# A hand-written interleaving of two transformer layers: where the second layer's feed-forward input, the first layer's gating and one state update stand in the order of work

## The chip, the cores and the metric

The kernel runs on one core of a Trainium2 chip. The metric is the time of one execution in device microseconds (us). A core has a matrix engine (PE, with its weight loads shown apart as PEld), a vector engine (DVE), an activation engine (ACT), a general engine (POOL) and DMA queues that the sync engine (SP) fills. Each engine works through its own list of instructions in order and waits on semaphores for the others.

## The reference

Eight sequences of 512 tokens with 128 features pass through two layers. Cut to what matters:

```python
x = L0_attn_x                                   # (8, 512, 128)
xn = layernorm(x)
s = causal_attention(xn)                        # 16 heads of 8, latent keys and values
g = silu(expert_ffn(xn))                        # 8 experts of 64, top 2 by gate
x = x + s * g
xn = layernorm(x)                               # called xn2 in the kernel
h = layernorm(xn) * gamma + beta                # called hn
k, v, q = h @ Wk.T + bk, h @ Wv.T + bv, h @ Wq.T + bq
# scan over the 512 tokens, W starts at 0:
#   y_t = W q_t ;  W = W - 0.01 * (W k_t - v_t) k_t^T
s = xn + y
g = silu(xn @ sign(weight).T)
x = x + s * g
```

The scan is done in four chunks of 128 tokens per sequence, each with a triangular inverse.

## The kernel before, in words

**Stages.** Up to five sequences are in work at once. In one iteration of the schedule one sequence (`second`) is normed and projected, the next (`nxt`) has its score maxima taken, the third (`cur`) has its attention done, the fourth (`prev`) goes through the second layer, and the fifth (`older`) is finished and stored. An iteration has four groups of ten units, written (group, unit) here, from (0, 0) to (3, 9), and a short group 4. A unit is an `s_unit` for `nxt` (scores into one half of `ps_s`, which DVE reduces to maxima in `cand`) and then an `e_unit` for `cur` (scores into one half of `ps_e`, which ACT exponentiates into `prob`). Each of `ps_s` and `ps_e` has two halves, so that unit n needs the `cand` (or `prob`) of unit n-2 to be finished.

**Order.** Between the units the table `PLAN` places all other pieces by hand. Every engine walks the same table and issues its own part of each piece, so that a piece's place sets its rank on all engines at once. `iteration` walks the table, `schedule` strings the iterations together, `numbers` counts the uses of a shared accumulator bank in that order, and the waits on `a_`, `c0_` and `c1_` semaphores come from these counts. Steady iterations are those in which `cur` is sequence 1 to 6; the last one has its own table, `LAST_PLAN`.

**Pieces that are touched.** `gb0` to `gb3`: PE spreads the gates (line 858, bank `ps_a`) and DVE multiplies the hidden activations by them (line 1441). `out`: 20 matmuls of the expert output (lines 865 and 867, `ps_a`), then ACT's tanh into `tG` (line 1238) and DVE's product (line 1446). `gt`: PE transposes the gates' parts, which POOL makes (lines 634 to 640) from DVE's `gate` (line 1436). `hn_norm` and `xn2_norm`: four DVE operations each (line 1394). `c_xn2t`: PE transposes `xn2` (line 969), ACT copies it out (line 1262). `c_ffn`: PE multiplies it by the sign weights (line 1074), ACT takes a tanh (line 1308), DVE finishes (line 1547). `c_vk`: PE projects values and keys into both banks `ps_c0` and `ps_c1` (line 997). `c_u2`: PE makes the third chunk's update (line 1099), ACT copies it into `u_sb` (line 1313), and `c_y2` uses it (line 1109). `pv0` to `pv2`: PE's product of probabilities and values for a group (line 950). `gelu`: ACT loads another function table and works over all of `hid` (line 1234); the next `prob` needs the first table again (line 1251). `ln2_stats` and `c_y3`: DVE's statistics and the last sum of the older sequence (lines 1377, 1382 and 1593). `c_out` on POOL: gate and add for the older sequence (lines 687 and 691).

Of the kernel before, what the change touches and what calls it, by code (L numbers as in the profile page):

```python
# [53 lines left out]

C0_PIECES = ("c_kt", "c_vk", "c_gram", "lev_a1", "lev_a2", "lev_a3", "lev_a4", "lev_a5", "lev_a6",
             "lev_d1", "lev_d2", "lev_d3", "lev_d4", "lev_d5", "c_u0", "c_u1", "c_u2", "c_u3", "c_r1", "c_r2", "c_r3", "c_y0", "c_y1", "c_y2")
C1_PIECES = ("c_ht", "c_qt", "c_vk", "c_gram", "c_xn2t", "c_ffn", "lev_d5", "lev_d6", "c_y3")


PLAN = {  # L60
    (0, 0): ["c_u3"], (0, 1): ["gb0"], (0, 2): ["ln2_stats", "c_y3"], (0, 4): ["ln2_rstd", "hn_norm"],
    (0, 6): ["pv0"], (0, 7): ["c_ht", "rn", "c_out"], (0, 8): ["gb1"], (0, 9): ["pv1", "c_kt", "c_qt"],
    (1, 0): ["load_x", "m_rows1"], (1, 1): ["c_vk", "gb2"], (1, 2): ["c_gram", "pv2"], (1, 3): ["logits"],
# [6 lines left out]
}  # L70
# [126 lines left out]
def two_layers(nc, x_in, W_dq, W_uq, W_dkv, W_uk, W_uv, W_o, w1_in, b1_in, w2_in, b2_in, cent_in, route_in,  # L197
               Wk_in, bk_in, Wv_in, bv_in, Wq_in, bq_in, gamma_in, beta_in, sign_in, out):
    SEQS, TOK, D = x_in.shape
    NT = TOK // P  # L200
# [5 lines left out]
    with ExitStack() as ctx:  # L206
# [299 lines left out]
        def _(pool):  # L506
# [112 lines left out]
            def token_norms(b):  # L619

                pool.wait_ge(S["ss_ready"], b.count(2, 2))
                g.tensor_scalar(ssm[:, :], ss[:, :], float(P), NORM_EPS * NORM_EPS, ALU.mult, ALU.max).then_inc(S["ssm_ready"], 1)
                pool.wait_ge(S["ssm_ready"], b.count(1, 1))
                after(pool, S["norm2"], NT * (b.c - 1))
                after(pool, S["cos_ready"], b.count(1, 0))
                g.tensor_tensor(rn[:, :], ssm[:, :], halfpow[:, 0, :], ALU.pow).then_inc(S["rn_ready"], 1)
# [53 lines left out]
            def c_out(b):  # L680
                r, o = second_layer(b)
                if b.c == SEQS - 1:
                    return
                pool.wait_ge(r.S["c1_emptied"], C1_NUMBER[b.c, "c_y3"] + 1)
                if b.c < SEQS - 2:
                    pool.wait_ge(r.S["c0_emptied"], C0_NUMBER[b.c + 1, "c_kt"] + 1)
                g.tensor_tensor(r.syg[:, :, :], r.sy[:, :, :], r.tF[:, :].rearrange("p (i d) -> p i d", i=NT), ALU.mult)\  # L687
                    .then_inc(r.S["syg_ready"], 1)
                pool.wait_ge(r.S["syg_ready"], o.count(1, 1))
                after(pool, r.S["stored"], o.count(16, 0))  # L690
                g.tensor_tensor(r.out_sb[:, :, :], x1[b.parity][:, :, :], r.syg[:, :, :], ALU.add).then_inc(r.S["out_ready"], 1)
# [26 lines left out]
        def _(pe):  # L718
# [245 lines left out]
            def c_xn2t(b):  # L964
                r, o = second_layer(b)
                c1_fill(b, "c_xn2t")
                pe.wait_ge(r.S["norm1"], o.count(NT, NT))
                for i in range(NT):
                    last = tr(r.ps_c1[:, tok(i)], r.xn2[:, i, :], ident[:, :])
                last.then_inc(r.S["c1_filled"], 1)  # L970

# [98 lines left out]
            def c_ffn(b):  # L1070
                r, o = second_layer(b)
                c1_fill(b, "c_ffn")
                for i in range(NT):
                    last = mm(r.ps_c1[:, tok(i)], r.xn2T[:, tok(i)], sgT[:, :], start=True, stop=True)
# [60 lines left out]
        def _(act):  # L1135
# [123 lines left out]
            def c_xn2t(b):  # L1259
                r, o = second_layer(b)  # L1260
                c1_full(b, "c_xn2t")
                copy(r.xn2T[:, :], r.ps_c1[:, :]).then_inc(r.S["c1_emptied"], 1)

# [379 lines left out]
```

## Time and profile before

| | |
|---|---|
| median of 3 runs | 617.68 us (611.39 to 619.85) |
| the profiled execution | 617.68 us, of which the span of instructions is 616.0 us |
| PE busy | 580.8 us, 94% |
| DVE busy | 391.8 us, 64% |
| ACT busy | 351.9 us, 57% |
| POOL busy | 171.7 us, 28% |
| mean granted TensorE clock | 0.982 |

A busy share counts the time in which at least one instruction of the engine is in work. The profiled execution is the median one, and 1.7 us of it lie outside its span. Times in the trace are counted from the start of the span. The unit (0, 0) of the steady iteration that serves as the example below starts its `e_unit` at 251.0 us, the next iteration's at 318.4 us.

### The profile page before, as it was taken

What the parts mean: (1) busy time and instruction counts of PE and PEld (TensorE: products, weight loads), DVE (VectorE), ACT (ScalarE), POOL (GpSimd) and SP (SyncE); (2) the same over time, 40 slices, a digit from 0 to 9 for tenths busy, and PEclk for the clock granted to TensorE, in tenths of its full rate; (3) what the DMA queues carried; (4) which work ended last, traced back from release to release, by engine and by line L of the source; (5) the groups of instructions that cost most, each with busy time, mean ns of one, the idle gap of its engine ahead of it and who ended that gap; (6) DMA issues with size and microseconds to landing.
All of it is one profiled execution on the core that took longest, in us unless ns stands there. A gap on an engine that the chain in (4) does not pass through costs nothing.

```text
span 616.0 us, 17485 instructions
## 1 busy us (share of the span) xinstructions
PE 580.8 (94%) x7289; PEld 389.4 (63%) x7289; DVE 391.8 (64%) x975; ACT 351.9 (57%) x679; POOL 171.7 (28%) x335
## 2 busy tenths in 40 slices
PE   7799989899998999899999999899998999799897
PEld 3345564567575766677666766678576777565565
DVE  4488765767667676867666685767666675412453
ACT  4412556755675476756675466656675476676231
POOL 7157022412224221432223230432224200311121
PEclk9999999999998999999998999799998999999899
DMA  4766293847252115410362014410361000000001
GB/s 113 162 153 132 44 84 90 157 63 63 74 116 48 43 29 114 97 43 10 87 118 60 10 45 98 95 44 5 83 128 41 10 12 1 26 18 2 3 3 35
DMA packets 58163, 39.42 MB, mean 64 GB/s; under 512 B 17957, under 2 KB 57988, under 8 KB 58084
## 3 DMA queue, kind: packets, MB, share of 16 engines
q1 hardware_dynamic: 58051, 38.29, 30.9%
q8 instruction: 58, 0.95, 0.7%
q14 instruction: 22, 0.17, 0.1%
q10 hardware_dynamic: 32, 0.01, 0.0%
HBM read 24.46 MB, written 9.96 MB: 56 GB/s over the span
## 4 chain that ended last, share of the span: by engine, by line
PE 79%; DVE 11%; ACT 4%; issue 2%; DMA 1%; POOL 1%; SPq 0%; DVEq 0%; POOLq 0%
PE ps_v L950 13%; PE ps_s L930 11%; PE ps_e L911 6%; PE ps_a L865 5%; PE ps_a L851 4%; PE ps_c L1015 4%; DVE cand L1457 4%; PE ps_e L903 3%; PE ps_e L907 3%; PE ps_e L738 3%; PE ps_a L820 3%; PE ps_s L933 2%; PE ps_c L1099 1%; PE ps_c L997 1%; PE ps_c L984 1%
## 5 line engine op out<-in xcount | busy, mean ns | idle before, releaser
L1457 DVE TENSOR_REDUCE cand<-ps_s 128x4 f32<-128x512 f32 (+1 forms) x320 | 213.4, 685 | 74.4 <-PE ps_s L933 45.4
L1251 ACT ACTIVATE prob<-ps_e 128x512 f32<-128x512 f32 x320 | 188.4, 598 | 97.2 <-PE ps_e L911 55.7
L930 PE MATMUL ps_s<-kst,qst 72*128 72x128 bf16 (+2 forms) x1024 | 126.4, 236 | 15.8 <-DVE cand L1457 12.0
L930 PEld LDWEIGHTS ps_s<-kst,qst 72*128 72x128 bf16 (+1 forms) x1024 | 72.1, 98 | 77.5 <-DVE cand L1457 36.5
L911 PE MATMUL ps_e<-qst,kst 75*128 75x256 bf16 (+3 forms) x416 | 105.3, 284 | 0.0
L950 PE MATMUL ps_v<-prob,vaug 128*32 128x512 f32 (+3 forms) x1024 | 90.6, 455 | 0.0
L903 PE MATMUL ps_e<-identb,negmask 128*128 128x150 bf16 (+3 forms) x320 | 73.2, 229 | 3.7 <-ACT prob L1251 3.3
L907 PE MATMUL ps_e<-qst,kst 128*128 128x128 bf16 x384 | 75.8, 223 | 0.0
L911 PEld LDWEIGHTS ps_e<-qst,kst 75*128 75x128 bf16 x416 | 40.9, 98 | 3.5
L738 PE MATMUL ps_e<-identb 128*128 128x512 bf16 x115 | 40.5, 408 | 1.9 <-POOL identb L520 1.9
L907 PEld LDWEIGHTS ps_e<-qst,kst 128*128 128x128 bf16 x384 | 38.4, 100 | 4.6 <-issue 0.3
L903 PEld LDWEIGHTS ps_e<-identb,negmask 128*128 128x128 bf16 x320 | 31.5, 99 | 14.6 <-ACT prob L1251 9.8
L950 PEld LDWEIGHTS ps_v<-prob,vaug 128*32 128x32 f32 x1024 | 24.1, 109 | 25.9 <-issue 20.3
L933 PE MATMUL ps_s<-negmask,identb 128*128 128x300 bf16 (+1 forms) x128 | 40.3, 315 | 0.0
L1015 PEld LDWEIGHTS ps_c<-second 32*32 32x32 f32 x2072 | 25.0, 107 | 21.3 <-issue 15.8
L649 POOL CAST mparts<-nm 128x32 bf16<-128x32 f32 x16 | 3.4, 211 | 121.8 <-DVE nm L1464 121.8
L865 PEld LDWEIGHTS ps_a<-w2s,hid 128*128 128x128 f32 x256 | 31.1, 192 | 7.1 <-issue 5.9
L1015 PE MATMUL ps_c<-second 32*32 32x32 f32 x2072 | 32.8, 194 | 2.5 <-DVE second L1520 1.6
L851 PE MATMUL ps_a<-xnT,w1s 128*128 128x512 f32 x64 | 33.5, 605 | 1.3 <-ACT hid L1230 0.8
L865 PE MATMUL ps_a<-w2s,hid 128*128 128x128 f32 x256 | 33.4, 283 | 0.7 <-ACT mrow L1243 0.7
L1230 ACT ACTIVATE hid<-ps_a,vecT 128x512 f32<-128x512 f32 x32 | 22.0, 687 | 17.1 <-PE ps_a L851 17.1
L687 POOL TENSOR_TENSOR second<-second,second_flat 128x512 f32<-128x512 f32 x7 | 8.9, 1266 | 60.2 <-ACT second_flat L1272 46.3
(340 smaller groups left out, 929.9 us busy)
## 6 DMA issues: line engine op xcount, KB each, us to landing
qst<-q_scratch SPq DMA_DIRECT2D x48, 192.0 KB
kst<-k_scratch SPq DMA_DIRECT2D x48, 192.0 KB
q_scratch<-qparts SPq DMA_DIRECT2D x24, 128.0 KB, 2.3
k_scratch<-kparts SPq DMA_DIRECT2D x24, 128.0 KB, 2.3
x_res<-in_L_attn_x_dram SPq DMA_DIRECT2D x8, 256.0 KB, 3.7
xn<-in_L_attn_x_dram SPq DMA_DIRECT2D x7, 256.0 KB, 3.5
out_dram<-second SPq DMA_DIRECT2D x7, 256.0 KB, 2.4
max_scratch<-mrow SPq DMA_DIRECT2D x16, 96.0 KB, 2.1
```

What stands on the lines that cost most here:

```text
L738: mm(ps_e[:, 1, :].rearrange("p (a c) -> p a c", c=P), identb[:, :], bcast(identb[:, :], 1, 4), start=True, stop=True, skip_group_check=True)
L851: mm(ps_a[:, :], w1s[:, 2 * c:2 * c + 2, :].rearrange("p e f -> p (e f)"), xnT[b.parity][:, :], start=True, stop=True)\
L865: mm(ps_a[:, tok(i)], hid[:, c, tok(i)], w2s[:, c, :], start=(i == 0 and c == 0), stop=False, skip_group_check=True)
L903: mm(diag, negmask[:, :], bcast(identb[:, masked:P], 1, len(todo)), start=True, stop=False, skip_group_check=True)
L907: last = mm(ps_e[:, bank, at:at + P], k[:, hd, tok(j)], q[:, hd, tok(j)], start=False, stop=True, skip_group_check=True)
L911: last = mm(ps_e[:, bank, at + own:at + TOK - P * j], k[0:SROWS, hd, tok(j)], q[0:SROWS, hd, P * j + own:TOK], start=False, stop=True, ski ...
L930: last = mm(ps_s[:, bank, w * n:w * (n + 1)], q[0:rows, hd, tok(i)], k[0:rows, hd, keys[0]:keys[1]], start=(n == 0), stop=True, skip_group ...
L933: last = mm(ps_s[:, bank, :].rearrange("p (a c) -> p a c", a=GH)[:, :, masked:P], identb[:, :], bcast(negmask[:, masked:P], 1, GH), start= ...
L950: last = mm(ps_v[32 * hh:32 * hh + 32, P * j:TOK], vaug[:, j, head_of(grp, hh), :], prob[:, u, o:o + TOK - P * j], start=(j == 0 and grp % ...
L1015: last = mm(bank[SQ * col:SQ * col + SQ, SQ * i:SQ * i + SQ], lhsT(row, col, i), rhs[SQ * row:SQ * row + SQ, i, :], start=True, stop=True, ...
L1251: af(prob[:, u, :], ps_e[:, u % 2, :], ACT.Exp).then_inc(S["e_emptied"], 1)
L1457: vec.tensor_reduce(cand[:, i, h0:h0 + FILLS * (len(hds) - 1) + 1:FILLS, S_SLOT[u]], ps_s[:, u % 2, :].rearrange("p (a c) -> p a c", a=len ...
```

## The change

Pieces move in `PLAN`. `gb1`, `gb2` and `gb3` go from (0, 8), (1, 1) and (1, 4) to (0, 4), (0, 6) and (0, 8). `out` goes from (1, 6) to (1, 1). `xn2_norm` goes from (1, 4) to (0, 7), `c_xn2t` from (1, 8) to (1, 0), `c_ffn` from (2, 1) to (1, 4), `gt` from (1, 9) to (1, 8). At (3, 9) `pv1` is put ahead of `c_u2`. `c_xn2t` uses bank `ps_c0` where it used `ps_c1`, and so `c_ffn` waits for that bank's release. Two waits of POOL are on `xn2_norm` now. `LAST_PLAN` moves `c_xn2t` and `c_ffn` forward in the last iteration. No instruction is added or removed.

```diff
-C0_PIECES = ("c_kt", "c_vk", "c_gram", "lev_a1", ...
+C0_PIECES = ("c_xn2t", "c_kt", "c_vk", "c_gram", "lev_a1", ...
-C1_PIECES = ("c_ht", "c_qt", "c_vk", "c_gram", "c_xn2t", "c_ffn", "lev_d5", "lev_d6", "c_y3")
+C1_PIECES = ("c_ht", "c_qt", "c_vk", "c_gram", "c_ffn", "lev_d5", "lev_d6", "c_y3")
 PLAN = {
...
-    (1, 4): ["yt", "gb3", "xn2_norm", "gates"], (1, 5): ["lev_a1", "gate_norm"], (1, 6): ["pv0", "out"], (1, 7): ["lev_d1"], (1, 8): ["c_xn2t"],
+    (1, 4): ["yt", "c_ffn", "gates"], (1, 5): ["lev_a1", "gate_norm"], (1, 6): ["pv0"], (1, 7): ["lev_d1"], (1, 8): ["gt"],
...
 LAST_PLAN = {
...
-    (2, 7): ["c_xn2t"], (3, 1): ["c_ffn"], (2, 9): ["pv1"], ...
+    (2, 8): ["c_ffn"], (2, 9): ["pv1"], ...
@@ token_norms (POOL)
-                after(pool, S["norm2"], NT * (b.c - 1))
+                after(pool, S["norm1"], NT * (b.c - 1))
@@ c_out (POOL)
-                    pool.wait_ge(r.S["c0_emptied"], C0_NUMBER[b.c + 1, "c_kt"] + 1)
+                    pool.wait_ge(S["norm1"], NT * (b.c + 2))
@@ c_xn2t (PE; ACT's copy likewise)
-                c1_fill(b, "c_xn2t")
+                c0_fill(b, "c_xn2t")
...
-                    last = tr(r.ps_c1[:, tok(i)], r.xn2[:, i, :], ident[:, :])
-                last.then_inc(r.S["c1_filled"], 1)
+                    last = tr(r.ps_c0[:, tok(i)], r.xn2[:, i, :], ident[:, :])
+                last.then_inc(r.S["c0_filled"], 1)
@@ c_ffn (PE)
                 c1_fill(b, "c_ffn")
+                pe.wait_ge(r.S["c0_emptied"], C0_NUMBER[b.c, "c_xn2t"] + 1)
```

Line numbers from 1073 on are higher by one in the changed kernel. Its order is shown at three places of a steady iteration.

DVE in group 0, from `ln2_stats` on, before (the `second` written at line 1593 is `c_y3`, the ones of line 1394 are `hn_norm`, `hid` is a `gb` piece):

```order
L1377 BN_STATS stats<-x_1 128x6 x4
L1382 BN_AGGR mv<-stats 128x2 x4
L1593 TENSOR_TENSOR second<-ps_c,second 128x512
L1457 TENSOR_REDUCE cand<-ps_s 128x4 x2
L1394 TENSOR_SCALAR second<-x_1,mv,rstd 128x128 x4
L1457 TENSOR_REDUCE cand<-ps_s 128x2 x4
L1441 TENSOR_TENSOR hid<-hid,ps_a 128x512
```

and in the changed kernel:

```order
L1594 TENSOR_TENSOR second<-ps_c,second 128x512
L1458 TENSOR_REDUCE cand<-ps_s 128x4 x2
L1442 TENSOR_TENSOR hid<-hid,ps_a 128x512
L1395 TENSOR_SCALAR second<-x_1,mv,rstd 128x128 x4
L1458 TENSOR_REDUCE cand<-ps_s 128x2 x2
L1442 TENSOR_TENSOR hid<-hid,ps_a 128x512
L1458 TENSOR_REDUCE cand<-ps_s 128x2
L1395 TENSOR_SCALAR second<-x_1,mv,rstd 128x128 x4
L1458 TENSOR_REDUCE cand<-ps_s 128x2
L1442 TENSOR_TENSOR hid<-hid,ps_a 128x512
```

A `gb` product now stands ahead of `hn_norm` and of the maxima of units 5 and 6, another behind them, and `xn2_norm` stands between the maxima of units 7 and 8.

ACT from the projection of q at (0, 9) to (1, 2), before (`mrow` is `m_rows1`):

```order
L1277 ACTIVATE second_flat<-ps_c,bq_lr 128x512
L1251 ACTIVATE prob<-ps_e 128x512
L1243 COPY mrow<-ps_a 96x512
L1251 ACTIVATE prob<-ps_e 128x512 x2
L1284 ACTIVATE second<-ps_c 32x128 x4
```

and in the changed kernel (line 1263 is the copy of `c_xn2t`, `tG` that of `out`):

```order
L1252 ACTIVATE prob<-ps_e 128x512
L1244 COPY mrow<-ps_a 96x512
L1263 COPY second_flat<-ps_c 128x512
L1252 ACTIVATE prob<-ps_e 128x512
L1239 ACTIVATE tG<-ps_a 128x512
L1252 ACTIVATE prob<-ps_e 128x512
L1285 ACTIVATE second<-ps_c 32x128 x4
```

The copy out of `ps_c0` stands behind `mrow`, and PE's `c_vk`, which writes that bank next, waits for it.

PE at (3, 9), before (32x384 and 32x128 are `pv1`, 32x256 is `pv2`, `rhs` is read by `c_u2`):

```order
L1099 MATMUL ps_c<-rhs,second 128x128
L950 MATMUL ps_v<-prob,vaug 32x384 x4
L950 MATMUL ps_v<-prob,vaug 32x128 x4
L950 MATMUL ps_v<-prob,vaug 32x256 x4
L1109 MATMUL ps_c<-u_sb,vk 128x128
```

and in the changed kernel:

```order
L950 MATMUL ps_v<-prob,vaug 32x384 x4
L950 MATMUL ps_v<-prob,vaug 32x128 x4
L1100 MATMUL ps_c<-rhs,second 128x128
L950 MATMUL ps_v<-prob,vaug 32x256 x4
L1110 MATMUL ps_c<-u_sb,vk 128x128
```

`c_u2` now stands between `pv1` and `pv2`, which followed each other.

## Rows read from the trace of the kernel before

**Rows 1.** The page: busy shares, and the granted clock in 40 slices

```profile
PE 580.8 (94%) x7289; PEld 389.4 (63%) x7289; DVE 391.8 (64%) x975; ACT 351.9 (57%) x679; POOL 171.7 (28%) x335
...
PEclk9999999999998999999998999799998999999899
```

**Rows 2.** Waits of PE and PEld: us in total, times, longest

```profile
PE ps_s L930 <- DVE cand L1457: 12.0, 10, 1.7
PE ps_e L903 <- ACT prob L1251: 3.3, 7, 1.0
...
PEld ps_v L950 <- issue: 20.3, 105, 0.3
```

**Rows 3.** Windows of group 0 in three iterations: length, busy time of PE, PEld, DVE, ACT, POOL, then PEclk

```profile
251.00:264.40 13.40, 11.61 (x116) 7.29 (x114) 10.51 (x27) 8.74 (x16) 6.64 (x9) 1.00 0.36 83
318.40:333.40 15.00, 13.22 (x117) 7.71 (x115) 10.67 (x27) 8.85 (x16) 6.67 (x9) 0.89 0.41 75
387.40:403.80 16.40, 14.61 (x115) 8.90 (x113) 10.74 (x27) 9.03 (x16) 6.61 (x9) 0.79 0.33 67
```

**Rows 4.** Timeline of DVE in group 0: start, length in us, what, [idle before]

```profile
254.12 0.86 DVE L1377 BATCH_NORM_STATS2 stats<-x 128x6 f32<-128x128 f32 x4
...
255.31 0.66 DVE L1593 TENSOR_TENSOR second<-ps_c,second 128x512 f32<-128x512 f32 x1
255.89 1.28 DVE L1457 TENSOR_REDUCE cand<-ps_s 128x4 f32<-128x512 f32 x2
257.08 1.11 DVE L1394 TENSOR_SCALAR second<-x,mv,rstd 128x128 f32<-128x128 f32 x4
258.11 1.88 DVE L1457 TENSOR_REDUCE cand<-ps_s 128x2 f32<-128x512 f32 x3
```

**Rows 5.** Timeline of PE in the same stretch

```profile
256.63 0.39 PE L930 MATMUL ps_s<-kst,qst 72*128 72x256 bf16 x2 [1.68 <-DVE cand L1457]
...
257.84 1.07 PE L950 MATMUL ps_v<-prob,vaug 128*32 128x512 f32 x8
258.85 0.39 PE L930 MATMUL ps_s<-kst,qst 72*128 72x256 bf16 x2
...
260.33 0.38 PE L858 MATMUL ps_a<-gT,pick 96*128 96x512 bf16 x1
260.55 0.39 PE L930 MATMUL ps_s<-kst,qst 72*128 72x128 bf16 x4
```

**Rows 6.** Timeline of ACT, then of PE, at (1, 0)

```profile
265.29 0.57 ACT L1243 COPY mrow<-ps_a 96x512 bf16<-96x512 bf16 x1
265.76 0.60 ACT L1251 ACTIVATE prob<-ps_e 128x512 f32<-128x512 f32 x1
...
265.43 1.46 PE L997 MATMUL ps_c<-wvk,second_flat 128*128 128x192 f32 x8
```

**Rows 7.** Timeline at (1, 5): DVE's gate, and POOL's last part of it

```profile
276.23 0.19 DVE L1436 TENSOR_TENSOR gate<-gm,grec 128x32 f32<-128x32 f32 x1
...
277.49 0.37 POOL L640 TENSOR_TENSOR gparts<-grest,gparts 128x96 bf16<-128x96 f32 x1
```

**Rows 8.** Timeline from (2, 1) to (2, 3), of PE, of DVE and of PE

```profile
285.15 1.05 PE L1074 MATMUL ps_c<-sgT,second_flat 128*128 128x128 f32 x8
...
286.45 0.68 DVE L1457 TENSOR_REDUCE cand<-ps_s 128x4 f32<-128x512 f32 x1
...
287.69 0.40 PE L930 MATMUL ps_s<-kst,qst 128*128 128x128 bf16 x4
```

**Rows 9.** Timeline from (3, 9) into the next iteration: PE, ACT, PEld

```profile
246.49 0.44 PE L1099 MATMUL ps_c<-rhs,second 128*128 128x128 f32 x2
246.86 1.50 PE L950 MATMUL ps_v<-prob,vaug 128*32 128x384 f32 x24
...
247.46 1.28 ACT L1234 ACT_TABLE_LOAD   x1
...
253.16 0.10 PEld L903 LDWEIGHTS ps_e<-identb,negmask 128*128 128x128 bf16 x1 [0.30 <-ACT prob L1251]
```

More of the change, by code:

```diff
@@ L53 @@
 A_PIECES = ("xnt", "q", "k", "logits", "gt", "m_rows0", "h0", "h1", "h2", "h3", "v", "gb0", "gb1", "gb2", "gb3", "m_rows1", "out")
-C0_PIECES = ("c_kt", "c_vk", "c_gram", "lev_a1", "lev_a2", "lev_a3", "lev_a4", "lev_a5", "lev_a6",
+C0_PIECES = ("c_xn2t", "c_kt", "c_vk", "c_gram", "lev_a1", "lev_a2", "lev_a3", "lev_a4", "lev_a5", "lev_a6",
              "lev_d1", "lev_d2", "lev_d3", "lev_d4", "lev_d5", "c_u0", "c_u1", "c_u2", "c_u3", "c_r1", "c_r2", "c_r3", "c_y0", "c_y1", "c_y2")
-C1_PIECES = ("c_ht", "c_qt", "c_vk", "c_gram", "c_xn2t", "c_ffn", "lev_d5", "lev_d6", "c_y3")
+C1_PIECES = ("c_ht", "c_qt", "c_vk", "c_gram", "c_ffn", "lev_d5", "lev_d6", "c_y3")
 PLAN = {
-    (0, 0): ["c_u3"], (0, 1): ["gb0"], (0, 2): ["ln2_stats", "c_y3"], (0, 4): ["ln2_rstd", "hn_norm"],
-    (0, 6): ["pv0"], (0, 7): ["c_ht", "rn", "c_out"], (0, 8): ["gb1"], (0, 9): ["pv1", "c_kt", "c_qt"],
-    (1, 0): ["load_x", "m_rows1"], (1, 1): ["c_vk", "gb2"], (1, 2): ["c_gram", "pv2"], (1, 3): ["logits"],
[2 rows of a table removed]
+    (0, 0): ["c_u3"], (0, 1): ["gb0"], (0, 2): ["ln2_stats", "c_y3"], (0, 4): ["gb1", "ln2_rstd", "hn_norm"],
+    (0, 6): ["pv0", "gb2"], (0, 7): ["c_ht", "xn2_norm", "rn", "c_out"], (0, 8): ["gb3"], (0, 9): ["pv1", "c_kt", "c_qt"],
+    (1, 0): ["load_x", "m_rows1", "c_xn2t"], (1, 1): ["c_vk", "out"], (1, 2): ["c_gram", "pv2"], (1, 3): ["logits"],
[2 rows of a table added]
     (2, 4): ["yt", "m_rows0"], (2, 5): ["lev_a4", "xnt"], (2, 6): ["pv0", "q", "lev_d4"], (2, 7): ["turned0"], (2, 8): ["lev_a5", "k"],
@@ L1260, in c_xn2t @@
                 r, o = second_layer(b)
-                c1_full(b, "c_xn2t")
-                copy(r.xn2T[:, :], r.ps_c1[:, :]).then_inc(r.S["c1_emptied"], 1)
+                c0_full(b, "c_xn2t")
+                copy(r.xn2T[:, :], r.ps_c0[:, :]).then_inc(r.S["c0_emptied"], 1)
             def c_ht(b):
```

8 rows, old and new, of tables (LAST_PLAN, PLAN) are left out of this document.

## The prediction

> **What bounds the kernel now.** I read the page first: PE is busy for 94% of the span, no other engine for more than 64%, and the clock shows digits under 9 in few slices [rows 1]. So the order of the other engines matters only where PE stands still or its clock falls. The table of waits says how much of that there is: PE's matmuls wait 12.0 us in all for DVE's maxima, the longest time 1.7 us, and 3.3 us for ACT's `prob` [rows 2]. The timeline places the longest: in each steady iteration PE stands for 1.68 us before the scores of unit (0, 5), because DVE does `ln2_stats` and `c_y3` ahead of the maxima of unit 3 [rows 4, 5]. Then I looked at group 0 in windows. The clean one, at 251, takes 13.4 us at a granted clock of 1.00. Three others (at 182, 318 and 458) take 15.0 us at 0.89, and one 16.4 us at 0.79, with the same work [rows 3]. So the long wait costs twice: 1.7 us itself, and in four of these five iterations part of what follows it runs at 1.2 GHz and not at 2.4, for 1.6, 1.6, 1.6 and 3.0 us more, 7.8 us in sum.
>
> **What the change takes away.** Nothing is added, so PE's work stays the same; I count waits only. The six steady iterations with a `prev` are the ones that count; times are those of the clean iteration at 251.
>
> 1. `gb1` goes to (0, 4), where PE stands anyway. One such matmul moves PE by 0.22 us (260.33 to 260.55) [rows 5], and that is hidden: -0.22. The wait itself stays, since DVE's chain up to `cand` of unit 3 is unchanged.
> 2. Two short waits in group 1 go with the pieces that caused them: `gb3` waited for the logits, and the scores behind `c_xn2t` for the maxima. I put both at 0.2 from the short entries of the timeline (estimate): -0.4.
> 3. The earlier `xn2_norm`, `c_xn2t`, `c_ffn` and `out` gain nothing by being early. No wait of PE in the table names their results: what they feed (POOL's gate and add) nobody waits for.
>
> **What it brings.** DVE issues full-width operations some 0.60 us apart when it has them in a row (255.89 to 257.08 for two) and the four of a norm take 1.03 (257.08 to 258.11) [rows 4].
>
> 4. Unit (0, 7). Its scores need `cand` of unit 5. Before, that runs from 258.11 to 258.80, and PE comes from `pv0` (257.84 and 1.01 later) at 258.85: the two meet exactly [rows 4, 5]. Now the product of `gb1` stands ahead of `hn_norm`, so that `cand` ends at 259.40. PE has `gb2` to do as well and comes at 259.07. Wait: 0.38.
> 5. Unit (0, 9) needs `cand` of unit 7, behind the product of `gb2`: DVE is done at 261.20, PE would come at 261.15. Wait: 0.09. `xn2_norm` and `gb3` fall behind it and are covered by `pv1`, `c_kt` and `c_qt`, where DVE had been idle. By the start of group 1 PE is 0.69 later, 0.22 of it moved work.
> 6. `c_xn2t` at (1, 0). ACT has no gap there: `mrow` and `prob` start 0.47 apart [rows 6]. The copy out of `ps_c0` comes between them, and `c_vk` can't write `ps_c0` until it is done. `mrow` would start at 265.98, the copy at 266.45 and end at 267.03; PE, with 0.69 and 0.44 for the transposes, comes to `c_vk` at 265.43 + 1.13 = 266.56. Wait: 0.52. In the bank `ps_c1` this copy was waited for by nothing close.
> 7. `out` leaves (1, 6). Its 4.1 us of pure matmul (20 matmuls behind each other) were DVE's time to catch up; now `c_ffn` stands in DVE's list at (1, 4), waits there for ACT's tanh, and behind it are the gates, two maxima and the gate norm. I lay these out one after the other: `cand` of unit (1, 6) ends at 282.18, PE wants unit (1, 8) at 281.92. Wait: 0.3.
> 8. `gt` at (1, 8) instead of (1, 9). From `gate` to the end of POOL's last part it takes 276.23 to 277.86, 1.63 us [rows 7]. By the same layout `gate` starts at 281.38, so the parts are ready at 283.06 and PE comes at 282.75. Wait: 0.3.
> 9. `c_ffn` leaves (2, 1). It takes PE 0.89 us (1.05, less the 0.16 by which the next matmul overlaps it). `cand` of unit (2, 1) ends at 287.13 and the scores that need it start at 287.69, 0.56 later [rows 8]. Without the 0.89 of cover PE comes 0.33 too soon, and the handover costs about 0.05 (from 256.58, when `cand` of unit 3 ends, to 256.63 [rows 4, 5]): 0.38. DVE's own part of `c_ffn` stands behind that `cand` and gives nothing back here. In the last of the six no sequence is normed at (2, 0), so this is paid five times.
> 10. `pv1` ahead of `c_u2` at (3, 9). `pv1` and `pv2` are one run of 1.50 now [rows 9]; split, PE starts such a run once more, and a start costs 20.3/105 = 0.19 for the load [rows 2] and as much again to get out of it. Between 0.19 and 0.38 I take 0.29. The second effect is larger but covered: `u_sb` is ready about 1.0 us later (`pv1` ahead of it), and with it ACT's table load, the gelu, the next table load and the first `prob`, on which PE waits already at 253.16 [rows 9]. PE then stands up to 0.9 us at (0, 2) instead of 0.2. That is paid out of the wait of 1.68 at (0, 5): DVE's chain depends on the scores of unit 3, which would be there by 255.2, before DVE wants them at 255.89. If that cover were gone, it would cost another 0.7 each, 4.2 us in all.
>
> Sum per iteration: -0.22 - 0.4 + 0.38 + 0.09 + 0.52 + 0.3 + 0.3 + 0.38 + 0.29 = 1.64. Six times, less 0.38: +9.5 us.
>
> **The clock.** What becomes of the 7.8 us is the open term, between 0 and all of it. The trace has one row of the same wait without the loss, at 251 [rows 3], and before each loss it shows the one wait of 1.68. In the changed kernel this wait is in two pieces, about 0.9 at (0, 2) and 0.75 at (0, 5), with 2 us of matmuls between, and the other waits are 0.1 to 0.5 and lie apart. No row of group 0 shows a fall of the clock behind waits of under 1 us. I take it that all of it is given back: -7.8. The Trainium skill has a rule that speaks against this, in "TensorE: Matmul & The Clock Gate", section "A second HAM failure mode: psum-queue depth-cycling": where TensorE idles for moments between groups of matmuls often enough, its clock swings between the two levels although no gap is long. By that rule the loss stays and the second rival below comes out. So far the trace speaks for the first reading: up to 500 us the clock line has four slices under 9 (the 13th, 22nd, 26th and 31st, each 15.4 us long), and each lies on a group 0 with the long wait, none on groups 1 to 3 with their short ones [rows 1].
>
> **Forecast.** 617.68 (the profiled execution, which is the median too, 616.0 of it span) + 9.5 - 7.8 = 619.4 us. In short: the change trades one long wait with a clock penalty for several short ones. `LAST_PLAN` moves two pieces to places where PE has waits of its own on both sides; I bound it by plus and minus 0.9, the length of `c_ffn`, and take 0.
>
> **The rivals.**
> - *The clock is given back and the short waits don't come.* They hang on differences of 0.1 to 0.5 us at six places, and I lay out DVE's and ACT's lists from a trace in which the pieces stand elsewhere. If only the swap's 0.29 is paid and the gains of points 1 and 2 come, the time is 617.68 - 7.8 + 6 x (0.29 - 0.62) = 607.9; with half of the waits, about 613. For it: four of the six waits are estimated from chains of more than five operations. Against it: points 4, 6 and 9 are read directly, each from two rows.
> - *Slower: the clock still falls.* The wait at (0, 2), the one at (0, 5) and the one at (0, 7) follow each other in some 6 us, and together they are 2.0 us, more than the one wait before. If the clock falls in as many iterations as now, nothing is given back: 617.68 + 9.5 = 627.2. The point from which it decides is the same share of idle PE as now, in two pieces. Against it stands the iteration at 251, which had all of the wait in one piece and kept its clock.
> - *The cover of point 10 fails.* Then 4.2 us come on top of the forecast, 623.6, or less with what the wait at (0, 5) still hides.
> - *The change does nothing that can be seen*, since nothing on PE's path waited for what comes earlier, and moved work is the same work: 617.7, with the same losses of clock.
>
> **How the numbers follow.** Forecast 0.42; clock back and few waits 0.27; clock still falls 0.18; cover fails 0.05; nothing seen 0.08. The three runs shown lie between 611.4 and 619.9, about as wide as these cases are apart, so that two kernels of this sort can hardly be told apart under 2%, which is 605.3 to 630.0 here. The range takes in the upper half of the first rival and all of the second: 609 to 627.5. Beyond 2%: faster needs all of the first rival and more, 0.03; slower needs the clock's fall and point 10's cover gone, or more falls than now (a double one as at 387 in every iteration), 0.03; 0.94 within.
>
> **What would show it.** In the profile after: the wait of the scores (line 930) on `cand` at (0, 5) under 1 us and not 1.68; a wait of PE on `prob` at (0, 2) near 0.9 and line 903's sum in the table of waits near 6 to 8 us where it is 3.3; the loads of `c_vk` waiting for ACT's copy (now line 1263) by 0.5; `gt` waiting for POOL; group 0 at clock 1.00 in most iterations, and then iterations of 69.0 us where the clean one now has 67.4. Wrong it would be made by a clock that behaves otherwise than in the one clean iteration, or by waits that PE's queue of weight loads hides or lengthens in a way that these rows don't show.

## The result, and the profile after

Over 20 runs of each kernel the changed one takes 621.25 us in the median (618.89 to 626.63), the one before 615.98 us (611.01 to 619.85). The ratio is 1.0093, with a 95% interval of 1.0067 to 1.0119: slower by just under 1%, and within the 2% that count as the same. The forecast was 619.4 in a range of 609 to 627.5. The profiled execution after took 621.56 us, 619.8 of it span, at a mean granted clock of 0.994, where the one of before had 617.68, 616.0 and 0.982. As a difference the forecast was +1.7 us; the two profiled executions differ by 3.9 and the two medians by 5.3.

The page of the changed kernel shows the same work on PE and a clock line with fewer dips:

```profile
PE 578.6 (93%) x7289; PEld 387.4 (62%) x7289; DVE 391.4 (63%) x975; ACT 353.0 (57%) x679; POOL 171.3 (28%) x335
...
PEclk9899999999999999999999999999999999899999
```

The four slices under 9 that lay on group 0 before [rows 1] are gone. PE is busy 2.2 us less than before [rows 1] although it does the same, because less of it is done at 1.2 GHz: a group 0 with a fall of the clock shows 13.22 us of PE where the clean one shows 11.61 [rows 3]. It would be more than 2.2, but part of the new waits is counted as busy: a whole iteration at full clock shows 66.3 us of PE after and 65.6 before, for the same 909 matmuls. The two dips that are left lie ahead of the steady iterations and behind them.

In windows of group 0 (length, busy time of the five engines, then PEclk), the iterations at 184, 254, 323 and 462 us are now alike:

```profile
184.35:198.43 14.08, 12.27 (x117) 7.46 (x115) 12.67 (x33) 9.41 (x18) 8.05 (x10) 1.00 0.38 77
253.63:267.70 14.07, 12.27 (x116) 7.46 (x114) 12.66 (x33) 9.40 (x18) 8.05 (x10) 1.00 0.33 73
...
461.70:475.77 14.07, 12.27 (x116) 7.46 (x114) 12.66 (x33) 9.41 (x18) 8.05 (x10) 1.00 0.43 77
```

Before, one was clean at 13.40 us and the others took 15.0 and 16.4 at 0.89 and 0.79 [rows 3]. Group 0 is 0.7 us longer than the clean one and never pays for the clock. The table of PE's waits (us in total, times, longest) says what it pays instead:

```profile
PE ps_s L930 <- DVE cand L1458: 9.1, 21, 1.1
PE ps_e L903 <- ACT prob L1252: 8.5, 13, 1.6
...
PE ps_c L997 <- ACT second_flat L1263: 2.2, 6, 0.4
...
PE ps_a L845 <- POOL gparts L640: 1.4, 7, 0.2
```

Before it was 12.0 in ten waits for the maxima and 3.3 in seven for `prob` [rows 2]; the last two rows are new, one wait in each of six or seven iterations. The timeline of PE in group 0, with the idle time in brackets, shows the one wait of 1.68 [rows 5] in its pieces:

```profile
256.47 0.21 PE L903 MATMUL ps_e<-identb,negmask 128*128 128x75 bf16 x1 [0.70 <-ACT prob L1252]
...
258.09 0.38 PE L858 MATMUL ps_a<-gT,pick 96*128 96x512 bf16 x1
259.29 0.39 PE L930 MATMUL ps_s<-kst,qst 72*128 72x256 bf16 x2 [0.82 <-DVE cand L1458]
...
261.50 0.39 PE L858 MATMUL ps_a<-gT,pick 96*128 96x512 bf16 x1
262.11 0.39 PE L930 MATMUL ps_s<-kst,qst 72*128 72x256 bf16 x2 [0.22 <-DVE cand L1458]
```

DVE's timeline in the same stretch is what the forecast laid out. A `gb` product (line 1442) stands ahead of `hn_norm` and of the maxima of units 5 and 6, and the two maxima that start at 261.36 are those for which PE waits again at 262.11:

```profile
257.97 0.66 DVE L1594 TENSOR_TENSOR second<-ps_c,second 128x512 f32<-128x512 f32 x1
258.55 1.28 DVE L1458 TENSOR_REDUCE cand<-ps_s 128x4 f32<-128x512 f32 x2
259.74 0.68 DVE L1442 TENSOR_TENSOR hid<-hid,ps_a 128x512 f32<-128x512 f32 x1
260.34 1.12 DVE L1395 TENSOR_SCALAR second<-x,mv,rstd 128x128 f32<-128x128 f32 x4
261.36 1.29 DVE L1458 TENSOR_REDUCE cand<-ps_s 128x2 f32<-128x512 f32 x2
```

At (1, 0) and (1, 1) ACT's copy (line 1263) holds `c_vk` (line 997). First ACT's timeline, then PE's:

```profile
268.65 0.57 ACT L1244 COPY mrow<-ps_a 96x512 bf16<-96x512 bf16 x1
269.12 0.59 ACT L1263 COPY second_flat<-ps_c 128x512 f32<-128x512 f32 x1
...
269.07 0.33 PE L911 MATMUL ps_e<-qst,kst 75*128 75x384 bf16 x1
269.77 1.57 PE L997 MATMUL ps_c<-wvk,second_flat 128*128 128x192 f32 x8 [0.37 <-ACT second_flat L1263]
```

And at (1, 8) two short waits follow each other. DVE's first operation here is its part of `c_ffn`, which comes late because of ACT's tanh; then the gate, POOL's last part of it, and PE:

```profile
281.91 0.69 DVE L1548 SCALAR_TENSOR_TENSOR second_flat<-second_flat,ps_c 128x512 f32<-128x512 f32 x1 [0.69 <-ACT second_flat L1309]
...
284.16 0.19 DVE L1437 TENSOR_TENSOR gate<-gm,grec 128x32 f32<-128x32 f32 x1
...
285.42 0.36 POOL L640 TENSOR_TENSOR gparts<-grest,gparts 128x96 bf16<-128x96 f32 x1
...
285.02 0.39 PE L930 MATMUL ps_s<-kst,qst 72*128 72x256 bf16 x2 [0.26 <-DVE cand L1458]
...
285.93 0.40 PE L845 MATMUL ps_a<-identb,gparts 128*96 128x128 bf16 x4 [0.22 <-POOL gparts L640]
```

**Where the time went.** From the start of one group's first `e_unit` (line 903 in the timeline) to the next group's, the iteration at 251 before and the one at 254 after compare as follows. The others that start between 182 and 393 us agree within 0.05 us where the clock holds (group 2 of one iteration is 0.2 longer in the changed kernel); the first and the last of the six have partly other pieces.

| us | group 0 | group 1 | group 2 | group 3 and 4 | iteration |
|---|---|---|---|---|---|
| before | 13.37 | 19.45 | 15.86 | 18.78 | 67.47 |
| after | 14.08 | 20.82 | 15.33 | 19.06 | 69.29 |

So 1.82 us more in an iteration. The six steady iterations with a `prev` sum to 409.3 us before and 412.7 after: 3.5 more (before rounding), which is 7.5 of clock given back (group 0 of the four iterations with falls, against the clean 13.37) and 11.0 of new waits. The start takes 1.9 more and the iteration ahead of these six 1.6 less, which makes the 3.8 by which the spans differ, but for 0.1. Of these 1.6, 1.2 are a wait that changed places: the step from (3, 9) is 3.64 where it was 4.81, and the one from (0, 1) behind it 2.58 where it was 1.41. Most of the other kernels show this too, the `gb` pieces alone for one, so it is not the change's. In the start no piece was moved; there this execution of the changed kernel has a fall of the clock at 27 us, and the one of before has none.

### The profile page after: what moved, and what is told of

Same layout as the page of the kernel before. It is cut to its first block, busy times and chain, and to the rows that moved or that the text cites. A ratio compares the mean times of both kernels' runs of the same rounds, so it can differ in the third digit from the quotient of the medians.

```text
span 619.8 us, 17493 instructions
## 1 busy us (share of the span) xinstructions
PE 578.6 (93%) x7289; PEld 387.4 (62%) x7289; DVE 391.4 (63%) x975; ACT 353.0 (57%) x679; POOL 171.3 (28%) x335
## 4 chain that ended last, share of the span: by engine, by line
PE 70%; DVE 16%; issue 5%; ACT 5%; POOL 3%; DMA 1%; SPq 0%; DVEq 0%; POOLq 0%
PE ps_v L950 10%; PE ps_s L930 9%; PE ps_a L865 5%; DVE cand L1458 5%; PE ps_e L911 5%; PE ps_a L851 4%; PE ps_c L1015 3%; PE ps_e L738 3%; PE ps_a L820 3%; PE ps_e L903 2%; PE ps_e L907 2%; PE ps_s L933 2%; PE ps_c L997 2%; PE ps_c L1100 2%; DVE stats L1378 2%
## 5 line engine op out<-in xcount | busy, mean ns | idle before, releaser
L930 PE MATMUL ps_s<-kst,qst 72*128 72x128 bf16 (+2 forms) x1024 | 125.1, 234 | 12.5 <-DVE cand L1458 9.1
L950 PE MATMUL ps_v<-prob,vaug 128*32 128x512 f32 (+3 forms) x1024 | 89.0, 444 | 0.0
L907 PE MATMUL ps_e<-qst,kst 128*128 128x128 bf16 x384 | 74.4, 220 | 0.0
L1447 DVE SCALAR_TENSOR_TENSOR gate_out<-tG,ps_a 128x512 f32<-128x512 f32 x8 | 5.5, 687 | 34.8 <-ACT tG L1239 34.8
```

What stands on the lines that cost most here:

```text
L907: last = mm(ps_e[:, bank, at:at + P], k[:, hd, tok(j)], q[:, hd, tok(j)], start=False, stop=True, skip_group_check=True)
L930: last = mm(ps_s[:, bank, w * n:w * (n + 1)], q[0:rows, hd, tok(i)], k[0:rows, hd, keys[0]:keys[1]], start=(n == 0), stop=True, skip_group ...
L950: last = mm(ps_v[32 * hh:32 * hh + 32, P * j:TOK], vaug[:, j, head_of(grp, hh), :], prob[:, u, o:o + TOK - P * j], start=(j == 0 and grp % ...
```

## The experiments

In the diffs each line shows only the entries of the table that differ. All lengths of groups are measured as in the table above, in steady iterations at full clock unless a fall is spoken of.

### The swap alone

```diff
 before, and:
-    (3, 9): ["c_u2", "pv1"],
+    (3, 9): ["pv1", "c_u2"],
```

> The kernel before with pv1 ahead of c_u2 at (3, 9) and nothing else. Theory (the swap is what gives the clock back, because it delays ACT's first prob and so cuts the 1.68 us wait at (0, 5) in two): steady iterations take 67.4 + 0.3 = 67.7 us, nearly all at clock 1.00; PE's waits are about 0.9 at (0, 2) and 1.0 at (0, 5); group 3 with its tail takes 19.0 us where it took 18.7; the whole is 617.7 - 7.8 + 1.7 = 611.6 us, some 4 to 6 under the kernel before. Rival (the clock came back because gb1 fills the wait and other work fills group 0, not through the swap): the clock falls in group 0 as often as before, and the time is 617.7 + 1.7 = 619.4 us. Second rival: the cover fails and the late prob costs 0.7 more per iteration (68.4).

Measured: 612.91 us in the median against 615.04 for the kernel before, ratio 0.9968 (0.9935 to 1.0001). Group 3 takes 19.06 (+0.28), group 0 13.38 as before. In windows of group 0 the clean one and the only one of the five from 183 us on that lost its clock:

```profile
251.26:264.64 13.38, 11.58 (x114) 7.31 (x112) 10.54 (x27) 9.36 (x18) 6.57 (x9) 1.00 0.38 79
386.77:401.60 14.83, 13.03 (x115) 7.95 (x113) 10.63 (x27) 9.36 (x18) 6.57 (x9) 0.88 0.34 69
```

and in the timeline of PE the wait of 1.68 is split:

```profile
254.11 0.21 PE L903 MATMUL ps_e<-identb,negmask 128*128 128x75 bf16 x1 [0.70 <-ACT prob L1251]
...
256.93 0.39 PE L930 MATMUL ps_s<-kst,qst 72*128 72x256 bf16 x2 [1.04 <-DVE cand L1457]
```

0.70 and 1.04 are together about what 1.68 was, group 0 is as long as before, and one iteration of five loses its clock where four did. The swap moves part of the idle time to (0, 2) and costs nothing in group 0; it costs 0.28 at (3, 9). Both rivals are out: the clock did not fall as often as before, and a clean iteration takes 67.75 and not 68.4. The gain in time, 0.3%, is not clear of 1 by its interval.

### The changed kernel without the swap

```diff
 after, and:
-    (3, 9): ["pv1", "c_u2"],
+    (3, 9): ["c_u2", "pv1"],
```

> The changed kernel with c_u2 ahead of pv1 again, as before the change. Theory: iterations without a fall of the clock take 69.3 - 0.3 = 69.0 us; the wait at (0, 5) is one piece again, 1.68 less the 0.22 of gb1, about 1.46, and the clock falls behind it in some iterations, 1.6 us each: 618 to 626 us. Rival (gb1 in the wait is what keeps the clock): no falls, clock 0.99 or more, and about 619.5 us, under the changed kernel.

Measured: 621.13 us, ratio to before 1.0105 (1.0051 to 1.0159). The wait at (0, 5) is one piece again, 1.46 long (the 1.68 less `gb1`). Group 0 in windows, with and without a fall:

```profile
186.15:201.34 15.19, 13.61 (x116) 8.35 (x114) 12.66 (x33) 8.88 (x16) 8.97 (x10) 0.89 0.37 73
256.27:270.34 14.07, 12.29 (x116) 7.42 (x114) 12.66 (x33) 8.77 (x16) 8.06 (x10) 1.00 0.38 77
```

Two of five iterations fell, for 1.1 us each where 1.6 was expected. The other pieces keep their price (groups 1 and 2 as in the changed kernel, group 3 18.78). So falls come back without the swap. That there are fewer than the four of before would be the work of `gb1` in the wait; one execution each does not show it.

### The `gb` pieces alone

```diff
 before, and:
-    (0, 4): ["ln2_rstd", "hn_norm"],
-    (0, 6): ["pv0"], (0, 8): ["gb1"],
-    (1, 1): ["c_vk", "gb2"], (1, 4): ["yt", "gb3", "xn2_norm", "gates"],
+    (0, 4): ["gb1", "ln2_rstd", "hn_norm"],
+    (0, 6): ["pv0", "gb2"], (0, 8): ["gb3"],
+    (1, 1): ["c_vk"], (1, 4): ["yt", "xn2_norm", "gates"],
```

> The kernel before with gb1, gb2, gb3 at (0, 4), (0, 6), (0, 8) and all else as before. Theory: one more DVE product ahead of cand of unit 5 makes PE wait at (0, 7) by 0.2 to 0.4, and group 0 (from the e_unit of (0, 0) to that of (1, 0), in an iteration at full clock) takes 13.9 us where it took 13.3; group 1 takes 18.8 or a little less where it took 19.5, since two gb matmuls (0.22 each) and one wait on the logits (0.2) are gone from it; together 0.1 less than before or the same. Rival (the moved gb pieces carry the added time of the change): group 0 and group 1 together take over 0.5 us more than before.

Measured, one run: 614.33 us, span 612.6. Group 0 takes 14.07 where the clock holds, group 1 19.01; three of five iterations fell, again with one wait of 1.46. Group 0 is exactly as long as in the changed kernel, so that `xn2_norm` at (0, 7), which is absent here, costs nothing. Group 1 loses 0.44, which is the two matmuls of 0.22 that left it and no more: taking `gb3` away saved no wait there. Together +0.26 per iteration, which is neither the theory's -0.1 to 0 nor the rival's 0.5: the theory missed by the waits it took to be gained in group 1.

### `c_xn2t` behind `c_vk`

```diff
 after, and:
-    (1, 0): ["load_x", "m_rows1", "c_xn2t"], (1, 1): ["c_vk", "out"],
+    (1, 0): ["load_x", "m_rows1"], (1, 1): ["c_vk", "c_xn2t", "out"],
```

> The changed kernel with c_xn2t at (1, 1) between c_vk and out, and not at (1, 0) ahead of c_vk. Theory (c_vk waits for ACT's copy out of the bank): PE's wait of line 997 on the copy is gone (it was 2.2 us over six), a wait of up to 0.2 for DVE's sum may stand in its place, and group 1 takes 20.4 to 20.6 us where it took 20.8. Rival (the bank does not matter, PE only shows elsewhere what DVE or ACT take): group 1 stays at 20.8.

Measured, one run: 619.17 us, span 617.4. Group 1 takes 20.41 (-0.41), all else is unchanged, and the row of `c_vk` waiting for ACT's copy is gone from the table of waits. So the wait hangs on the copy standing ahead of `c_vk`: with the same transposes and the same copy behind it, PE's two units (1, 0) and (1, 1) take 0.43 less.

### `gt` back, and `out` back

```diff
 after, and:
-    (1, 8): ["gt"], (1, 9): ["pv1", "lev_a2"],
+    (1, 9): ["pv1", "lev_a2", "gt"],
 and in the second kernel also:
-    (1, 1): ["c_vk", "out"], (1, 6): ["pv0"],
+    (1, 1): ["c_vk"], (1, 6): ["pv0", "out"],
```

> The changed kernel with gt at (1, 9) again, behind lev_a2. Theory (gt came before POOL had its parts): PE's wait of line 845 on POOL is gone and group 1 takes 20.6 us where it takes 20.82. Rival (PE then waits as long for DVE's maxima at (1, 9)): 20.8.

> The run with gt at (1, 9), with out at (1, 6) again behind pv0. Theory (the 4 us of out at (1, 6) were the cover of c_ffn's and the gates' chain on DVE): the wait for cand of unit (1, 6), 0.26, goes as well, and group 1 takes 20.3 us. Rival (the place of out does not matter for PE, and the added time of group 1 is from c_xn2t and c_ffn alone): group 1 as in the run with gt back, 20.6.

Measured, one run each: 617.77 us (span 616.0) with `gt` back, 619.60 (617.9) with both. With `gt` at (1, 9) group 1 takes 20.53 (-0.29), and the wait for POOL's parts is gone. With `out` at (1, 6) too it takes 20.88: 0.35 *more*, where I had expected it to give the wait at (1, 7) back (20.3), and the rival no change (20.6). It does that: the step from (1, 7) to (1, 8) goes from 1.32 to 1.00. But the next one goes from 0.60 to 1.19, and DVE's and PE's timelines say why:

```profile
282.85 0.69 DVE L1447 SCALAR_TENSOR_TENSOR gate_out<-tG,ps_a 128x512 f32<-128x512 f32 x1 [3.63 <-ACT tG L1239]
283.45 0.68 DVE L1458 TENSOR_REDUCE cand<-ps_s 128x2 f32<-128x512 f32 x1
...
284.20 0.40 PE L930 MATMUL ps_s<-kst,qst 72*128 72x128 bf16 x4 [0.49 <-DVE cand L1458]
```

`out`'s own product on DVE (line 1447) stands ahead of the maxima and waits 3.63 us for PE's 20 matmuls and ACT's tanh. PE reaches the scores before those maxima are done. In the kernel before, `c_xn2t` stood just there, and its transposes covered part of this (argued: the kernel before with `out` alone moved was not run). In the changed kernel, then, the place at (1, 6) is no net gain: it covers one wait and brings a larger one.

### `c_ffn` back

```diff
 after, and:
-    (1, 4): ["yt", "c_ffn", "gates"],
+    (1, 4): ["yt", "gates"], (2, 1): ["c_ffn"],
```

> The changed kernel with c_ffn at (2, 1) again. Theory (c_ffn covers DVE's late cand at (2, 1)): group 2 takes 15.86 us again where it takes 15.33, group 1 takes 19.7 (0.89 of work and the 0.26 wait gone), so that the two together are 35.5 to 35.6 where they are 36.15. Rival (a matmul block is a matmul block, its place gives nothing): together 36.15.

Measured, one run: 619.76 us, span 618.0. Groups 1 and 2 take 19.45 and 15.86, together 35.31 against 36.15: -0.84 per iteration, somewhat more than the 0.55 to 0.65 of the theory. The step from (1, 7) to (1, 8) falls from 1.33 to 1.00, the next from 1.14 to 0.89, and the one from (2, 2) to (2, 3) from 2.05 to 1.67. So `c_ffn` in DVE's list at (1, 4) was the cause of the wait at (1, 7) and of most of the one of `gt`, and at (2, 1) its matmuls were cover, as the forecast had it. The whole time did not follow (the other five of the six steady iterations give 4.1 us, the span 1.8), because the first steady iteration took 72.4 us and not 69.5; more on this below.

### `c_y3` out of DVE's way, in two ways

The wait of 1.68 in the kernel before comes from `c_y3` and the statistics ahead of the maxima. These two kernels leave all else alone and move `c_y3` behind them:

```diff
 before, and in the first kernel:
-    (0, 2): ["ln2_stats", "c_y3"], (0, 6): ["pv0"], (0, 7): ["c_ht", "rn", "c_out"], (0, 8): ["gb1"],
+    (0, 2): ["ln2_stats"], (0, 6): ["pv0", "c_y3"], (0, 7): ["rn", "c_out"], (0, 8): ["c_ht", "gb1"],
 in the second:
-    (0, 2): ["ln2_stats", "c_y3"],
+    (0, 2): ["ln2_stats"], (0, 5): ["c_y3"],
```

> The kernel before with c_y3 at (0, 6) where it was at (0, 2), and c_ht at (0, 8) where it was at (0, 7); nothing of the change is in it. Theory (the 1.68 us wait at (0, 5) and the fall of the clock behind it come from c_y3 standing ahead of cand of unit 3 on DVE): the wait becomes 1.1 us, group 0 takes 12.8 us where it took 13.4, the clock stays at 1.00 in nearly all iterations, steady iterations take 66.9, and the whole 617.7 - 7.8 - 3 = 606 to 609 us. Rival (DVE only moves its late point: what is not waited for at (0, 5) is waited for at (0, 7), and c_ht comes too late for c_kt): group 0 stays at 13.4, and only the clock is gained, 611 us.

> The kernel before with c_y3 at (0, 5) where it was at (0, 2), and c_ht left at (0, 7). Theory (at (0, 6) c_y3 lost its cover, made PE wait 0.1 before (0, 7) and c_ht 0.15; at (0, 5) it stands behind cand of unit 5, which the scores of (0, 7) need): the wait at (0, 5) is 1.1 us again, the scores of (0, 7) come some 0.4 us earlier than in the kernel before, group 0 takes 13.1 to 13.2 us at full clock where it takes 13.37, and the whole is 608 to 609 us. Rival (cand of unit 6, now behind c_y3, is waited for at (0, 8) by as much): group 0 stays at 13.3 to 13.4 and the time is that of the run with c_y3 at (0, 6), 609.7.

Measured: the first 609.68 us (608.0 to 612.24) against 613.03 for the kernel before beside it, ratio 0.9927 (0.9894 to 0.996); the second 610.16 (608.18 to 612.9) against 616.8, ratio 0.9896 (0.9866 to 0.9926). These two are faster than both kernels of the case. Windows of group 0, one of the first and one of the second:

```profile
252.54:265.85 13.31, 12.11 (x114) 7.25 (x112) 10.54 (x27) 8.98 (x16) 6.58 (x9) 1.00 0.38 80
```

```profile
252.47:265.83 13.36, 12.06 (x114) 7.25 (x112) 10.55 (x27) 8.91 (x16) 6.56 (x9) 1.00 0.38 83
```

PE's timeline of the first has the wait as one piece, but short:

```profile
257.61 0.39 PE L930 MATMUL ps_s<-kst,qst 72*128 72x256 bf16 x2 [1.08 <-DVE cand L1457]
```

So the theories failed (group 0 of 12.8, and of 13.1 to 13.2) and the rivals came out (13.3 to 13.4, and only the clock gained). The wait is 0.60 shorter and group 0 hardly at all (13.31 and 13.35 against 13.37). The step from (0, 4) to (0, 5) does lose 0.60, but `c_y3`'s own matmuls now stand where PE has no idle time, DVE does it between maxima that PE needs soon, and `c_ht` or its successor is pushed: +0.34 and +0.20 in the first kernel, +0.19, +0.15 and +0.24 in the second. What makes them faster is, within 0.4 us, the clock: no steady iteration fell. The mean clocks of the runs that make up the ratios say the same: 0.9961 against 0.9886 for the kernel before beside it is 4.6 us of 613, and the ratio is 4.5; in the second, 0.9970 against 0.9869 is 6.2, and the ratio is 6.4.

### Three pieces back at once

```diff
 after, and:
-    (1, 0): ["load_x", "m_rows1", "c_xn2t"], (1, 1): ["c_vk", "out"],
-    (1, 4): ["yt", "c_ffn", "gates"], (1, 8): ["gt"], (1, 9): ["pv1", "lev_a2"],
+    (1, 0): ["load_x", "m_rows1"], (1, 1): ["c_vk", "c_xn2t", "out"],
+    (1, 4): ["yt", "gates"], (1, 9): ["pv1", "lev_a2", "gt"], (2, 1): ["c_ffn"],
```

> The changed kernel with gt at (1, 9) and c_ffn at (2, 1) again, and c_xn2t between c_vk and out. Theory (the waits are separate and add up): a steady iteration takes 69.28 - 0.84 - 0.41 - 0.30 = 67.7 us, which leaves the swap's 0.29 over the kernel before; with the clock at 1.00 in most iterations the whole is 619.4 - 9.2 = 610 to 613 us, under the kernel before. Rival (they stand in for each other, so that taking three away uncovers the next): 68.2 us or more, and 614 or more.

Measured: 617.88 us (615.53 to 620.88), ratio 1.003 (0.9998 to 1.0061). The steady iteration takes 67.91 us, 1.37 less than in the changed kernel; the three alone had given 0.41, 0.29 and 0.84, which is 1.54, so 0.17 were counted twice (`gt` waits in part because of `c_ffn`). By the iteration it lies between the theory (67.7) and the rival (68.2 or more), nearer to the theory; the whole time came out as the rival had it. Two things are in it. The mean clock of the ten runs is 0.992, where the profiled one, the fastest of them, has 0.997. And in the first steady iteration, which takes 70.8 us, PE's timeline has this:

```profile
146.05 0.34 PE L1015 MATMUL ps_c<-second 32*32 32x32 f32 x17
148.75 0.32 PE L1015 MATMUL ps_c<-second 32*32 32x32 f32 x15 [2.37 <-issue]
```

PE stops for 2.37 us in the middle of a run of 32 matmuls and no semaphore is awaited. The kernel with `c_ffn` back has the same in the same iteration, 2.22 long, with a fall of the clock behind it. The other kernels don't have it. The list of DMA queues, first from 126.2 to 145.7 us and then from 145.7 to 147.6, says what goes with it (packets, MB, share of the 16 engines):

```profile
q1 hardware_dynamic: 6146, 1.66, 81.7%
...
q1 hardware_dynamic: 431, 0.11, 62.7%
q8 instruction: 1, 0.02, 5.6%
```

For 20 us the queue marked "instruction" brings nothing, while the kernel's own transfers fill the other queue; then one packet of 16 KB comes, from 145.8 to 147.5, and PE goes on 1.2 us behind it (1.5 in the kernel with `c_ffn` back). Since the packet before it PE had started 491 matmuls and weight loads (496 there); between two such packets it starts 404 at most anywhere else in the twelve kernels. So PE most likely had no instructions left. Why the packet came late is not shown.

## Why the prediction was right, and where not

**The whole.** "One long wait with a clock penalty for several short ones" is what the traces show, and with nearly the forecast's sizes: the waits brought 11.0 us where 9.5 were forecast, and the clock gave 7.5 back where 7.8 were (the windows of the forecast were cut to the tenth; from `e_unit` to `e_unit` the four falls cost 1.47, 1.51, 1.55 and 2.99). The profiled execution came out 2.2 us above the forecast; 1.5 of it are the waits. The terms were large and of opposite sign, so the rise itself was forecast at less than half of its size.

**Group by group.** The forecast had +0.69 for group 0, +0.29 for group 3 and +0.66 for groups 1 and 2 together; measured are +0.71, +0.28 and +0.84. By points, from steps between two units that stand in one kernel and not in the other:

| point | forecast | measured | from |
|---|---|---|---|
| 1, 4, 5: `gb1` hidden, the waits at (0, 7) and (0, 9) | +0.25 | +0.26 | `gb` pieces alone: 0.70 in group 0 less the 0.44 that left group 1 |
| 2: `gb3`'s wait in group 1 gone | -0.2 | 0 | `gb` pieces alone |
| 2: the scores' wait behind `c_xn2t` gone | -0.2 | -0.23 | three back, against before, at (1, 8): 0.67 less, 0.44 of it transposes |
| 6: `c_vk` waits for ACT's copy | +0.52 | +0.52 at its start, 0.63 by the end of its unit | both traces; the step from (1, 1) is 2.54 with `out` back and 1.91 with the `gb` pieces alone |
| 7: the scores of (1, 8) wait | +0.3 | +0.33 | `c_ffn` back |
| 8: `gt` waits for POOL | +0.3 | +0.29 | `gt` back |
| 9: no cover at (2, 1) | +0.38 | +0.38 | `c_ffn` back, at (2, 2) |
| 10: the swap | +0.29 | +0.28 | swap alone, and its absence |

- *Points 1, 4 and 5* held. The step from (0, 6) to (0, 7) grew by 0.60, which is `gb2`'s 0.22 and the 0.38 of point 4. The bracket in the timeline shows only 0.22 idle there; the rest is in the handover, so that here the step between units measures the wait better than its bracket.
- *Point 2* is the step that failed. "`gb3` waited for the logits ... I put both at 0.2 from the short entries of the timeline": group 1 lost the 0.44 of its two matmuls and nothing else when they left. The step from (1, 4) did lose 0.16 more than the matmul, and the one from (1, 5) grew by 0.15: the next maxima were then waited for. A short idle entry ahead of an instruction is no gain when the next one waits as long in its place. These 0.2 are about what the measured 1.82 per iteration lies above the forecast's 1.64.
- *Point 3* held for what it says: nothing was gained by the results being early. `xn2_norm` in group 0 neither gained nor cost.
- *Point 6*: `c_vk` starts 0.26 us after its unit's `e_unit` before and 0.78 after, 0.52 more. Undoing it gives 0.41 back of the 0.63; about 0.2 stay, since the copy and the transposes are not free in the other place either.
- *Point 7* had the size right and its reason half wrong. "`out` leaves (1, 6). Its 4.1 us of pure matmul ... were DVE's time to catch up": with `out` back the wait at (1, 7) does go, but a larger one comes at (1, 8), and the sum is 0.35 worse. What brings the wait is `c_ffn` in DVE's list; without it the step is 1.00 wherever `out` stands. With `c_ffn` and `gt` back and `c_xn2t` behind `c_vk`, 0.26 for the `gb` pieces and 0.28 for the swap would make 0.54 over the iteration of before, and 0.44 are measured. That leaves about -0.1 for `out` and `c_xn2t` at (1, 1) and `xn2_norm` at (0, 7) together; they were not taken apart.
- *Point 9* was right for (2, 1). The whole price of `c_ffn`'s move, 0.84, is what the forecast had in points 7, 8 and 9 (0.98), less some 0.1 that `gt` at (1, 8) costs without it as well.
- *Point 10*: the wait at (0, 2) is 0.70 (0.9 was forecast), the one at (0, 5) 0.82 (0.75). The step from (0, 1) to (0, 2) grew by 0.65, and the one from (0, 4) to (0, 5) fell by 0.63. The cover held to within 0.02 us, and in the swap alone group 0 is as long as before.

**The clock.** The step "I take it that all of it is given back" held in the profiled execution. Over the runs the gain is less, because the profiled execution of before was one with many falls: its mean clock is 0.982, that of 17 runs of the same kernel beside the first four experiments 0.9875, and that of the 21 runs after 0.9953. Of some 616 us that is (0.9953 - 0.9875) x 616 = 4.8 us and not 7.5. With 11.0 of waits it makes 6.2, and the ratio of 1.0093 is 5.7 us. To start from the mean clock of many runs would have been the better ground; with the three times shown alone it could not be had. That the absolute forecast lies within 1.9 us of the median after is therefore in part luck: it started from 617.68, 1.7 above the later median of the kernel before.

The experiments give the clock's side in one table. The falls are counted in the profile of a single execution (five iterations from the second steady one on); beside them stands the mean clock of all runs of that kernel:

| kernel | idle of PE up to (0, 5) | iterations that fell, of 5 | mean clock (runs) |
|---|---|---|---|
| before | 1.68 in one | 4 | 0.9875 (17) |
| `gb` alone | 1.46 in one | 3 | 0.989 (1) |
| without the swap | 1.46 in one | 2 | 0.9912 (4) |
| swap alone | 0.70 and 1.04 | 1 | 0.9942 (12) |
| after | 0.70 and 0.82 | 0 | 0.9953 (21) |
| `c_y3` later, first | 1.08 in one | 0 | 0.9961 (12) |
| `c_y3` later, second | 1.08 in one | 0 | 0.9970 (6) |
| three back | 0.71 and 0.81 | 0 | 0.9922 (10) |

The longest single wait goes with the falls better than the sum does: the swap alone has as much idle time as before and a fourth of the falls. Between 1.04 and 1.08 in the table no order can be read, with one execution each. The last row does not fit by its mean clock: its waits in group 0 are those of the changed kernel, and its ten runs lie lower. It has the stop of 2.4 us as well, and in the kernel with `c_ffn` back the clock fell behind that stop; whether this explains its runs is not shown. The four single runs with `c_xn2t` moved, `gt`, `out` or `c_ffn` back have no fall in the five iterations either. Where it falls the clock goes from 2.4 to 1.2 GHz, and that costs 1.1 to 1.6 us each time (15.19 against 14.07 without the swap, 14.88 against 13.37 before). The rule that the forecast names from the Trainium skill, "TensorE: Matmul & The Clock Gate", section "A second HAM failure mode: psum-queue depth-cycling", would have kept the loss in the changed kernel, with more short idle moments than before. The trace goes against it here: seven waits of 0.2 to 0.8 us in an iteration, and no fall in six. That says nothing of shorter or denser ones.

**The rivals.** "The clock is given back and the short waits don't come" fell by the waits: all six came. "The clock still falls" fell by the windows; its price, 627.2, lies above every run after. The cover of point 10 did not fail. "Nothing seen" fell by the interval, which leaves 1 out.

## What to carry to other kernels

Before moving a piece in an order that several engines walk, write down for each place what it covers there and whom it delays on every engine; in this kernel pieces that nobody waited for were moved earlier, gained nothing, and took cover from places that used it. A long wait of the matrix engine can be worth shortening or breaking up even if the same idle time comes back elsewhere, because the clock may fall behind it: the two best kernels here cut the wait from 1.68 to 1.08 us and gained 0.7 and 1.0%, with group 0 as long as before. Change one entry at a time: the swap alone was at least as fast as before, and the other moves beside it made the whole slower.

## What the runs showed of the hardware

- The same code, in the same execution, kept its clock in one iteration and lost it in the next, and the kernel before lies between mean clocks of 0.980 and 0.994 in 51 runs. A single profile of such a kernel can be 3 to 4 us off the mean for this reason alone. With a longer single wait more iterations fell (0 of 5 at 0.82, 1 at 1.04, 2 and 3 at 1.46, 4 at 1.68, but 0 at 1.08); what decides a given iteration is not shown.
- PE stopped once for 2.2 to 2.4 us inside a run of small matmuls, with no semaphore awaited, in two of the twelve kernels and in the first steady iteration only, and went on 1.2 and 1.5 us behind a late packet of the instruction queue. It costs a fifth of what all the change's new waits do.
- The first `e_unit` starts between 58.6 and 63.1 us in these kernels, though ahead of it all of them have the same 291 matmuls on PE and 92 instructions on DVE. Two things make up most of this spread of 4.5 us. In three kernels (the two with `c_y3` later, and three back) a wait of PE at line 764 ends at 15.6 us and not at 13.5 to 14.0. And the clock falls near 27 us in eight of them: the three with neither start at 58.6 to 59.1, those with one of the two at 60.4 to 61.1, those with both at 62.5 and 62.6, and the one with a fall twice as long at 63.1. The spread is nearly as large as the effect of the change, and only comparing iterations inside the traces gets below it.
